# Layer 0's score maxima in one sequence of steps half a pair of heads ahead, and 384 instead of 256 columns of the exponentials added by GpSimd

## What is computed

```python
def _L0_xattn_ref(x, context, Wq, Wk, Wv, Wo, bo):      # HEADS = 8, DIM_HEAD = 64
    q = (x @ Wq).reshape(B, Nq, HEADS, DIM_HEAD)
    k = (context @ Wk).reshape(B, context.shape[1], HEADS, DIM_HEAD)
    v = (context @ Wv).reshape(B, context.shape[1], HEADS, DIM_HEAD)
    sim = jnp.einsum('bihd,bjhd->bhij', q, k) * SCALE
    attn = jax.nn.softmax(sim, axis=-1)
    out = jnp.einsum('bhij,bjhd->bihd', attn, v)
    return out.reshape(B, Nq, HEADS * DIM_HEAD) @ Wo + bo
...
def bitnet_linear(x, W, b):                             # layer 1
    i_scale = jnp.maximum(jnp.max(jnp.abs(x)), 1e-08) / 127.0
    qx = jnp.clip(jnp.round(x / i_scale), -128.0, 127.0)
```

## Time and profile before

| what | value |
|---|---|
| median of three executions | 1639.65 us |
| the profiled execution, its own time | 1638.51 us |
| its span in the trace (first to last instruction) | 1636.8 us |
| PE busy / DVE busy / ACT busy / POOL busy | 93% / 79% / 69% / 30% |
| maxima of pair 0 before the loop | 59.6 to 126.8 us |
| the loop of layer 0 (4 pairs) | 126.8 to 1003 us |
| the loop of layer 1's cross-attention | 1338 to 1590 us |

### The profile page before, as it was taken

How to read it: one execution, slowest core, us unless ns; L and a number is a source line. 1 busy time by engine, 2 the same in 40 slices (tenths; PEclk the granted TensorE clock), 3 DMA queues, 4 the chain that set the end, 5 groups by cost and what they waited for, 6 DMA issues and landing times.

```text
span 1636.8 us, 27033 instructions
## 1 busy us (share of the span) xinstructions
PE 1530.1 (93%) x9058; PEld 548.9 (34%) x9058; DVE 1286.3 (79%) x2319; ACT 1126.0 (69%) x1541; POOL 490.9 (30%) x488
## 2 busy tenths in 40 slices
PE   6889999999999999999999998899997979999986
PEld 4312333333333333333333223344444612222223
DVE  6898987879977779878789897877775666787766
ACT  6787777768877778777777786655554469676643
POOL 6303343334543334433300010345451012233100
PEclk9759999999999999999999998999999979999998
DMA  4000000000200000000010000111100000000000
GB/s 135 7 1 11 1 1 1 1 2 11 54 1 2 1 1 1 3 1 11 20 32 3 1 1 19 37 46 45 45 27 1 1 1 2 0 1 1 1 14 13
DMA packets 14834, 22.79 MB, mean 14 GB/s; under 512 B 1990, under 2 KB 11766, under 8 KB 14710
## 3 DMA queue, kind: packets, MB, share of 16 engines
q1 hardware_dynamic: 14710, 21.22, 4.6%
HBM read 20.69 MB, written 0.52 MB: 13 GB/s over the span
## 4 chain that ended last, share of the span: by engine, by line
PE 69%; issue 11%; DVE 9%; POOL 5%; ACT 4%; DMA 0%; POOLq 0%; SPq 0%; DVEq 0%; ACTq 0%
PE PS L2167 22%; PE PS L2153 15%; PE PS L2511 6%; PE PS L2199 5%; POOL WRK L734 5%; PE PS L2498 3%; DVE KNB L1382 3%; PE PS L2020 2%; PE PS L2012 2%; PE PS L2116 2%; PE PS L2540 2%; PE PS L2450 1%; PE PS L2435 1%; PE PS L2004 1%; ACT KNB L959 1%
## 5 line engine op out<-in xcount | busy, mean ns | idle before, releaser
L1382 DVE CUSTOM_DVE_ANT_0 KNB<-PS,KNB 128x512 f16<-128x512 f32 (+2 forms) x500 | 338.5, 690 | 152.4 <-PE PS L2199 106.9
L1432 DVE TENSOR_TENSOR WRK<-WRK 128x768 f32<-128x768 f32 (+3 forms) x400 | 425.2, 1063 | 15.3 <-ACT WRK L933 8.4
L933 ACT ACTIVATE WRK<-PS 128x1024 f32<-128x1024 f32 (+1 forms) x408 | 401.4, 1022 | 47.6 <-PE PS L2153 39.2
L2167 PE MATMUL PS<-WRK,V 128*64 128x512 f32 (+1 forms) x1632 | 395.7, 605 | 0.0
L708 POOL TENSOR_TENSOR WRK<-WRK 128x256 f32<-128x256 f32 x300 | 274.7, 916 | 395.6 <-ACT WRK L933 394.6
L959 ACT ACTIVATE KNB<-PS 128x512 f16<-128x512 f32 (+2 forms) x306 | 180.9, 591 | 77.8 <-PE PS L2199 77.2
L2344 PE MATMUL PS<-WRK,KNB 128*128 128x512 f16 x828 | 188.3, 381 | 7.1 <-POOL WRK L734 2.7
L2167 PEld LDWEIGHTS PS<-WRK,V 128*64 128x64 f32 (+1 forms) x1632 | 99.3, 136 | 192.7 <-issue 154.5
L2153 PE MATMUL PS<-KNB,KB 64*128 64x512 f16 (+1 forms) x1224 | 156.5, 377 | 0.0
L2153 PE MATMUL PS<-Q,KB 64*128 64x512 f16 (+1 forms) x1224 | 153.0, 377 | 0.0
L1162 ACT ACTIVATE WRK<-PS 128x1024 f32<-128x1024 f32 x100 | 102.4, 1024 | 51.1 <-PE PS L2498 47.6
(11 more groups left out here) (379 smaller groups left out, 1834.2 us busy)
## 6 DMA issues: line engine op xcount, KB each, us to landing
V<-in_moe_w_dram SPq DMA_DIRECT2D x44, 192.0 KB, 2.4
KNB<-in_ctx_fm_dram SPq DMA_DIRECT2D x6, 384.0 KB, 8.4
X<-in_ctx_fm_dram SPq DMA_DIRECT2D x12, 192.0 KB, 2.4
CTX<-in_ctx_fm_dram SPq DMA_DIRECT2D x6, 384.0 KB, 3.9
BW<-in_bit_w_dram SPq DMA_DIRECT2D x1, 960.0 KB, 9.8
PWK<-in_pair_w_dram SPq DMA_DIRECT2D x4, 192.0 KB, 2.8
XT<-in_x_fm_dram SPq DMA_DIRECT2D x1, 512.0 KB, 5.0
X<-in_x_tm_dram SPq DMA_DIRECT2D x1, 512.0 KB, 12.0
```

The lines of the kernel that those rows point to most:

```text
L933: e.activation(PR[0:r, u % 2, b, :], bank(2 * b, 2 * b + 2, slice(0, r)), ACT.Exp).then_inc(S("exp"), 1)
L1382: return e.tensor_tensor_reduce(diffs, sums, diffs, 0.5, NEG, ALU.add, ALU.max, accum_out=out)
L1432: e.tensor_tensor(total, total, part, ALU.add).then_inc(S("acc"), 1)
L2167: ins = e.matmul(PS[h * HD:(h + 1) * HD, 4, :], V[0:r, j, h * HD:(h + 1) * HD], PR[0:r, unit_no(hf, i) % 2, b, h * HALF:(h + 1) * HALF], s ...
```

## The change

Layer 0's maxima become one sequence of 7 x 52 = 364 steps (`NSTEP`), ordered by half-pass: those of pair 0's second half come first, in pair 0's own slots, then each half-pass in turn, so a half's maxima are ready about half a pair ahead. Alone, before the loop, only pair 0's first half is made: 26 double steps instead of 52. Steps now run in every slot up to slot 11 of the last pair, two to a slot, with a third in slots 3, 4, 5 of pair 0 and in slots 32 to 44 (even), 48 and 50 of pairs 0 to 2. `shifts` (with the diagonals) runs once per half-pass, at the start of the slot after its last step: slots 25 and 48, 21 and 44, 16 and 40, and 12 of the last pair. Queries and key sums go through bank 5 and other slots. DVE adds 640 columns, GpSimd 384, now also in hf 6; so GpSimd's reductions over rows are moved: the first ahead of hf 6's additions, the second between those of its units 19 and 20, the third behind them. `CHAIN` starts one slot later, and its first rounded copy is kept in another buffer.

```diff
-SHARE = 3 * T // 4
+SHARE = 5 * T // 8
...
-STEPS = full_then_rest(NFULL, lambda t: (0, 1), 3)
-NM = len(STEPS)
+TILES_H = NT // 2
+STEPS = [[(c, [t], g) for c in range(NFULL) for t in range(TILES_H * u, TILES_H * u + TILES_H) for g in range(2)]
+         + [(NFULL, list(range(TILES_H * u + a, TILES_H * u + b)), g) for a, b in ((0, 3), (3, TILES_H)) for g in range(2)] for u in range(2)]
+NM = len(STEPS[0])
...
-ALONE0 = full_then_rest(NDC - 1, lambda t: (0, 1), 6)
+ALONE0 = [(d, [t], g) for d in range(NDC - 1) for t in range(TILES_H) for g in range(2)] + [(NDC - 1, [0, 1, 2, 3], g)
+                                                                                     for g in range(2)]
...
+POOL_HALVES = 2 * PAIRS - 1
-    return SHARE if hf < 2 * (PAIRS - 1) else T
+    return SHARE if hf < POOL_HALVES else T
...
-THIRD_M = (32, 36, 40, 44, 48)
-def micro_steps(s):
-    if not FIRST_M <= s <= LAST_M:
-        return []
-    a = 2 * (s - FIRST_M) + sum(t < s for t in THIRD_M)
-    return list(range(a, a + 2 + (s in THIRD_M)))
...
+NSTEP = NM * (2 * PAIRS - 1)
+WITH_VALUES = (32, 34, 36, 38, 40, 42, 44, 48, 50)
+THIRD_M = [(3, 4, 5) + WITH_VALUES] + [WITH_VALUES] * (PAIRS - 2) + [()]
+def first_step(p, s):
+    return min(2 * (p * SLOTS + s) + sum(len(x) for x in THIRD_M[:p]) + sum(t < s for t in THIRD_M[p]), NSTEP + 1)
...
+def ready(p, s):
+    return half_done(*divmod(p * SLOTS + s - 1, SLOTS)) if p * SLOTS + s else None
+def split_steps(p, s):
+    steps = micro_steps(p, s)
+    return steps[:1], steps[1:-1], steps[1:][-1:]
...
+K16_AT = (6, 9, 13, 16, 20, 23, 25)
...
-        at[0] += [("wk", n), ("q", (n, 0)), ("q", (n, 1))]
-        at[1] += [("wv", n), ("kd", (n, 0)), ("ks", (n, 0))]
-        for c in range(1, NMC):
-            at[4 + 3 * c].append(("kd", (n, c)))
-            at[5 + 3 * c].append(("ks", (n, c)))
+        at[0].append(("wk", n))
+        at[1] += [("wv", n), ("q", (n, 0))]
+        at[2].append(("q", (n, 1)))
+        for c, k in enumerate(K16_AT):
+            at[k].append(("kd", (n, c)))
+            at[k + 1].append(("ks", (n, c)))
...
-CHAIN = [("none",)] * 2
+CHAIN = [("none",)] * 3
...
+            def largest(i):
+                e.wait_ge(S("ax"), i + 1)
+                e.partition_all_reduce(AM[:, i:i + 1], AX[:, i:i + 1], P, RED.max).then_inc(S("am"), 1)
+            for hf in range(POOL_HALVES):
+                if hf == POOL_HALVES - 1:
+                    largest(0)
                 for i in range(NU):
                     for b in tiles_of(i):
                         add_up(hf, i, b)
-            for i in range(3):
-                e.wait_ge(S("ax"), i + 1)
-                e.partition_all_reduce(AM[:, i:i + 1], AX[:, i:i + 1], P, RED.max).then_inc(S("am"), 1)
+                    if hf == POOL_HALVES - 1 and i == CHAIN.index(("max", 1)) - 1:
+                        largest(1)
+            largest(2)
...
-            def magnitude(p, steps):
+            def magnitude(steps):
                 for m in steps:
-                    if m == NM:
+                    if m == NSTEP:
                         continue
-                    c, tiles, _ = STEPS[m]
+                    c, tiles, _ = step(m)
                     w = HALF if c < NFULL else len(tiles) * REST
-                    n = micro_base(p) + m
+                    n = STEP0 + m
                     e.wait_ge(S("x_ps"), n + 1)
-                    if m >= 2:
-                        e.wait_ge(S("mx"), n - 1)
+                    e.wait_ge(S("mx"), n - 1)
                     e.activation(MC[:, m % 2, 0:w], PS[:, 6, 0:w], ACT.Abs).then_inc(S("x_cp"), 1)
...
+                    e.wait_ge(S("k_ps"), PAIRS * NKP)
...
-            def shifts(done, parts, rows):
+            def shifts(hf, done, parts):
+                u, rows = hf % 2, slice(hf % 2 * NT, hf % 2 * NT + NT)
                 e.wait_ge(S("mx"), done)
-                link(e.tensor_reduce(NEGM[:, 0:rows], MXP[:, 0:rows, 0:parts], X, ALU.max, negate=True))
-            def diagonals(u, heads, head_rows):
-                for h in range(heads):
-                    row = h * head_rows + 4 * u
+                link(e.tensor_reduce(NEGM[:, rows], MXP[:, rows, 0:parts], X, ALU.max, negate=True))
+                if hf >= 2:
+                    e.wait_ge(S("sc"), tile_no(hf - 2, 0, 0) + 1)
+                for h in range(2):
+                    row = u * NT + h * TILES_H
                     ins = e.tensor_tensor(DIAG[:, h, 4 * u:4 * u + 4, :],
                                           ident16[:, :].unsqueeze(1).to_broadcast([P, 4, P]),
                                           NEGM[:, row:row + 4].unsqueeze(2).to_broadcast([P, 4, P]), ALU.mult)
                 ins.then_inc(S("diag"), 1)
...
-                    if s == SLOTS - 1 and p + 1 < PAIRS:
-                        shifts(micro_base(p + 1), NMC, 2 * NT)
-                        e.wait_ge(S("sc"), tile_no(2 * p, 0, 0) + 1)
-                        diagonals(0, 2, NT)
+                    first, mid, last = split_steps(p, s)
+                    if ready(p, s):
+                        shifts(ready(p, s), STEP0 + ready(p, s) * NM, NMC)
                     before = divmod(unit_no(hf, i) - 1, NU)
                     if before[0] >= 0:
                         add_up(*before, 0)
-                    maximum(p, first)
+                    maximum(first)
                     if before[0] >= 0 and len(tiles_of(before[1])) > 1:
                         add_up(*before, 1)
-                    maximum(p, mid)
-                    maximum(p, last)
+                    maximum(mid)
+                    maximum(last)
...
-            def max_steps(p, steps):
+            def max_steps(steps):
                 for m in steps:
-                    if m < NM:
-                        e.wait_ge(S("k16"), (p + 1) * 2 * NMC + 2 * STEPS[m][0] + 2)
+                    if m < NSTEP:
+                        e.wait_ge(S("k16"), half_step(m)[0] // 2 * 2 * NMC + 2 * step(m)[0] + 2)
                         if m:
-                            e.wait_ge(S("x_cp"), micro_base(p) + m)
+                            e.wait_ge(S("x_cp"), STEP0 + m)
                     if m > 1:
-                        e.wait_ge(S("mx"), micro_base(p) + m - 1)
-                    if m < NM:
-                        max_half(p, m, 0, 6, "x_ps")
+                        e.wait_ge(S("mx"), STEP0 + m - 1)
+                    if m < NSTEP:
+                        max_half(m, 0, 6, "x_ps")
                     if m:
-                        max_half(p, m - 1, NH, 7, "y_ps")
+                        max_half(m - 1, NH, 7, "y_ps")
...
+                else:
+                    e.wait_ge(S("x_cp"), STEP0 + NSTEP)
+                    e.wait_ge(S("mx"), STEP0 + NSTEP)
```

More of the change, by code:

```diff
@@ L93, in rows_of, with micro_steps, half_step, step @@
     return P if j < KT - 1 else TAIL
[L97 to L112 removed]
+NSTEP = NM * (2 * PAIRS - 1)
[3 more added lines that the diff above has]
+    return min(2 * (p * SLOTS + s) + sum(len(x) for x in THIRD_M[:p]) + sum(t < s for t in THIRD_M[p]), NSTEP + 1)
+def micro_steps(p, s):
+    return list(range(first_step(p, s), first_step(*divmod(p * SLOTS + s + 1, SLOTS))
+                      if p * SLOTS + s + 1 < PAIRS * SLOTS else NSTEP + 1))
+def half_step(m):
+    return 1 + m // NM, m % NM
+def step(m):
+    h, k = half_step(m)
+    return STEPS[h % 2][k]
+def half_done(p, s):
+    done = [m // NM for m in micro_steps(p, s) if m and m % NM == 0]
+    return done[0] if done else None
+def ready(p, s):
[3 more added lines that the diff above has]
+    return steps[:1], steps[1:-1], steps[1:][-1:]
 def inside(x):
     return x[0] == "dk"
[L120 to L121 removed]
+STEP0 = len(ALONE0)
+K16_AT = (6, 9, 13, 16, 20, 23, 25)
 def items_of(p):
@@ L158 @@
             "bits": "bit_dve"}
-BANK_OF = {("q", 0): 6, ("q", 1): 7, ("kd", 0): 6, ("ks", 0): 7}
-def bank_of(x):
-    return BANK_OF.get((x[0], x[1][1]), 5) if x[0] in ("q", "kd", "ks") else 5
-BANK5 = [x for p in range(PAIRS) for s in range(SLOTS) for x in ITEMS[p][s] if x[0] in FREED_BY and bank_of(x) == 5]
+BANK5 = [x for p in range(PAIRS) for s in range(SLOTS) for x in ITEMS[p][s] if x[0] in FREED_BY]
+for _p in range(PAIRS - 1):
+    for _c, _k in enumerate(K16_AT):
+        _steps = [m for m in range(NSTEP) if step(m)[0] == _c]
+        _last = max(m for m in _steps if half_step(m)[0] == 2 * _p + 1)
+        _first = min(m for m in _steps if half_step(m)[0] == 2 * _p + 2)
+        assert first_step(_p, _k) > _last + 1 and first_step(*divmod(_p * SLOTS + _k + 2, SLOTS)) <= _first
 def freed(x):
@@ L708, in add_up @@
                     e.tensor_tensor(total, total, part, ALU.add).then_inc(S("acc_pool"), 1)
-            for hf in range(2 * (PAIRS - 1)):
+            def largest(i):
[4 more added lines that the diff above has]
+                    largest(0)
                 for i in range(NU):
@@ L1414, in _ @@
             max_alone(0, ALONE0, True)
-            shifts(len(ALONE0), NDC, 2 * NT)
```

(12 more changed lines are left out.)

63 lines of the change are left out of this document (22 added, 41 removed).

## The result

The change makes the kernel slower: 1667.35 us (median of four runs, 1665.92 to 1668.95) against 1639.46, a ratio of 1.0172 (95% interval 1.0154 to 1.0189), 27.9 us. Forecast were 8.5 us more and a range up to 1659. The direction was right, the size was not.

A forecast was written before the change was run, and what follows sets the result against it. The prediction took DVE to pace layer 0's maxima alone and PE its loop. Its terms summed to +8.5 us on the span's 1636.8, giving a forecast median of 1648 us, range 1633 to 1659.

The forecast's parts named there:

- Fewer columns on DVE: Both layers' additions: 128 columns fewer on DVE save about 0.13 us an addition where PE waits; -3.0 us, bounds -8 to +3.
- What bounds the kernel: Layer 0: DVE paces the maxima alone, PE paces the loop; a step costs PE 0.215 us, plain slots stay at 3.70 us.
- the steps' 12.0 us of PE's work: Layer 0's loop: 56 more step slots at 0.215 us each, hidden by nothing; +12.0 us.
- The stage alone and the start of the loop: Before and at layer 0's loop start: fewer maxima alone, -31.7 us; third step waiting for ACT and longer low clock, +0.9.
- More third steps: Loop slots with a third step: waits beyond PE's work, 0.54 us each with values, 0.6 without; +8.2 us, bounds +4 to +11.
- The shifts among the steps: Six loop slots: shifts ahead of additions and maxima make PE's next step wait; +5.5 us, bounds 0 to +8.
- Steps beside the rounding: Last pair: ACT's two |x| beside its rounding exceed PE's time in six slots; +2.0 us, bounds +1 to +5.
- GpSimd's changes of code: Last pair: switching between additions and reductions stalls the core twice, +4.6 and +7.0 us; +11.6 together, bounds 0 to +15.
- the rival without a price: GpSimd in the last pair: changing code costs nothing, nor does the clock behind it; -6.1 us, 1633.5, chance 0.17.
- half of the small terms absorbed: Layer 0's loop: code's price stands, but DVE catches up behind shifts and the clock doesn't drop; 1639.7 us, chance 0.18.
- DVE's waits go after all: Both layers: narrower additions free the steps, -12 instead of -3; with half the shifts' cost 1636 us, chance 0.05.
- GpSimd paces every slot: Layer 0's loop: GpSimd's longer additions reach 4.0 us and slow some 90 plain slots; +27 us, 1675, chance 0.05.

The follow-up runs named there:

- e5_both: The changed kernel with GpSimd's part at 256 columns, no additions by it in the last pair's first half, and reductions behind its last addition: 1647.8 us.
- e2_share768: The changed kernel with GpSimd's part back at 256 columns in both layers: 1659.5 us.
- e3_before640: The kernel before the change with GpSimd's part at 384 columns and nothing else: 1642.4 us, ratio 1.0015.
- e11: e5_both with only one tile of the shifts' diagonals written instead of eight, from the second pair's first half on: 1642.5 us.
- e4_split: The changed kernel with each half's diagonals written in four pieces of two tiles over up to four slots, a few halves excepted: 1663.5 us.
- e9_thirds: The kernel before with as many steps, begun two slots later in each pair, and third steps in nine slots with values instead of five: 1646.2 us.
- e1_code: The changed kernel with no GpSimd additions in the last pair's first half and its three reductions one after the other behind its last addition: 1653.8 us.
- e7_extra: The kernel before with one more GpSimd reduction, between its additions for units 11 and 12 of the third pair's first half: 1646.2 us.

## Why the prediction failed in size

The path from before by e5_both and e2_share768 to after splits the 27.9 us, beside the prediction's terms:

| part | predicted | measured |
|---|---|---|
| order of the steps: alone, head, PE's work, thirds, shifts, last pair | -3.1 | +8.4 (e5_both) |
| changes of code with the clock behind them | +14.6 | +11.8 (e2 - e5), 13.5 with 384 columns |
| 384 columns for 256 | -3.0 | +7.8 (after - e2) |

Two of the three rows failed. The changes of code came nearly as forecast; the order of the steps cost 11.5 us more and the columns 10.8 us more than forecast.

**Fewer columns on DVE** is the step whose sign was wrong: -3.0, bounds -8 to +3, measured +7.8 (in the kernel before, e3_before640, some 3). The sentence "In layer 0 some waits around the weight sums of pair 0 and the start of pairs go" was the mistake; they came, at just these places. Of the 9.7 us that e2_share768 gains in layer 0's loop, 3.2 are the clock's drops in the two late slots, which a wait of 1.95 or 2.02 us in place of 2.09 and 2.08 no longer brings, 1.7 the first stall, and the rest 0.35 to 0.4 us in each of ten slots like that of e3, with 0.1 to 0.2 in some others. Layer 1's -2.2 was right in sign. I had rows of the collision, 1.21 us for 0.73, and named it in this term ("GpSimd's longer additions collide with DVE's more") without giving it a price. The Trainium skill (SBUF — State Buffer, Who interferes with whom) says that a VectorE instruction with two SBUF inputs and a GpSimd one that reads SBUF exclude each other, and that whichever comes second blocks until the first ends. The 1.55 for 0.82 us of e3 agrees. The 0.72 us tile of e11 waits in the same way, though it has one SBUF input besides its column of scalars; the same section of the Trainium skill counts tensor_scalar among the instructions that can hold both ports. By the exclusive rule GpSimd's longer additions are VectorE's waits, and the term would have had the other sign.

**What bounds the kernel** was read rightly: the plain slots stay at 3.70 us (364.73 to 368.43), the steps' 12.0 us of PE's work came, and nothing hid them.

**The stage alone and the start of the loop**: -30.5 for -30.8, but by two errors that cancel. The seeds start 32.5 us earlier (94.35 for 126.83), where -31.7 was forecast, and from there to the first values it takes 10.04 us for 8.03, +2.0 where +0.9 was forecast. In e5_both that stretch is 11.41 us and in e4_split 12.42, at granted clocks of 0.69 and 0.50 for 0.77 in the changed kernel, so this part moves by 1 to 2 us with how long the lower clock lasts.

**Work moved into the loop** stands in no term. "Seeds, queries, keys and values are as many as before" is true of the whole kernel, but before, four query matmuls (130.58) and four of key sums (133.90) stood ahead of the first values. Now two of the query matmuls and the key sums stand behind them: 1.06 and 4 x 0.215 us, +1.9 in the loop.

**More third steps**: right at 0.54 us each in slots with values (e9_thirds, 6.7 for 6.5). In the first pair's slots without values (from 109.21, 114.14 and 119.03) the 4.9 us for 3.70 are 1.0 beyond PE's work each, not 0.6, since PE waits both for a maximum and for |x| (0.27 and 0.35 us in the last of them).

**The shifts among the steps**: the six slots were priced at 6.9 us, "a short queue may absorb some" made it +5.5, bounds 0 to +8. Against slots of the same kind without shifts (5.38, 5.91 and 5.42 us late, 3.71 and twice 4.24 early), the late ones cost 1.8, 1.3 and 1.5 us in e5_both and the early ones 0.7, 1.0 and 0.5, which is 6.8 in all: with 256 columns the prices were right, and nothing absorbed any of it. With all of the change it is 3.4, 2.9 and 1.7 and then 1.1, 1.2 and 0.7, 10.9 in all. So this step failed in two ways. "Four diagonals take 2.50 us, so two are 1.25" took a price from a place where GpSimd stands idle and used it beside GpSimd's 384 columns, where two took up to 2.09 us in the late slots. And I put the lower clock only behind the two long stalls, though a wait of 2.1 us brought it twice here.

**Steps beside the rounding**: +3.0 for +2.0 in the changed kernel, and +4.7 in e5_both, where VectorE adds all 1024 columns in these slots.

**GpSimd's changes of code**: confirmed by removal (e1_code), by its slots (15.1 for 14.6) and by doing it once to the kernel before (e7_extra, 6.9). With 256 columns it costs 11.8: the first stall's slot is 9.32 us for 10.98, the second's 11.40 for 11.99, but 0.6 more follows in the slot behind it, and VectorE's additions of 1024 columns, which take GpSimd's place in that half, cost 2.6 us in the step slots there, for 1.7 with 384 columns. The prediction's ground against the rival without a price was weaker than it says: the row at 978.15 is a TENSOR_SCALAR, which GpSimd had not run before in that trace, so it couldn't show that "code that had run all along" costs as much to come back to. The runs show it (6.67 to 7.75 us). The rival without a price for code is out, and so is the one with half of the small terms absorbed, and "DVE's waits go after all"; "GpSimd paces every slot" is out by the plain slots.

**The order's row as a whole**: in e5_both layer 0's loop grows by 37.3 us for the 27.7 of its four terms. Steps 12.0, third steps 10.0, shifts 6.8, rounding 4.7 and the moved work 1.9 make 35.4; the other 1.9 are spread over slots and assigned to nothing. With the 2.1 us by which the first values came late, that is most of the 11.5 us.

**Between the layers** (+3.0 us with the same code) the traces show where a part of it goes. 24 us behind the last values of layer 0, the same code before and after:

```profile
1024.07:1028.07 4.00, 3.48 (x16) 1.13 (x14) 3.62 (x19) 3.70 (x6) 0.00 (x0) 1.00 0.18 52
1051.39:1055.39 4.00, 3.96 (x11) 1.28 (x9) 3.55 (x24) 1.42 (x2) 0.00 (x0) 0.59 0.14 46
```

The granted clock is 1.00 before and 0.59 after, and PE falls behind by about 1 us there. The other traces fall in line: where the clock is 0.93 or more at this place, the stretch between the layers takes 343.6 to 344.0 us, at 0.82 to 0.90 it takes 344.1 to 344.7, at 0.73 345.4 (e11_one_diag), at 0.52 to 0.62 346.3 to 347.0 (e1_code, the changed kernel and e2_share768).

**Left open**: what decides how long the lower clock lasts there and before the first values, with the same code. And why the clock fell after waits of 2.08 and 2.09 us and not after 1.92 to 2.02: the runs show it, and not why.
